# Two score matmuls side by side: the order of TensorE's work in the expert stage of an attention and mixture-of-experts kernel

## The chip, the cores and the metric

The kernel runs as one program on 1 core of a Trainium2 chip. The metric is the device time in microseconds (us), median of three runs. TensorE (PE) multiplies matrices, VectorE (DVE) and ScalarE (ACT) read its results from PSUM, GpSimd (POOL) works in SBUF, and SyncE (SP) issues the transfers. Each engine takes its own instructions in program order and waits on semaphores for the others.

## The reference

The input `x` has 2 batches of 512 rows of 128. Four residual blocks follow each other; the change lies in the second, a mixture of eight attention experts:

```python
def expert_step(acc, params):
    qw, qb_, kw, kb_, vw, vb_, ow, ob_, g = params
    q = (x @ qw.T + qb_).reshape(B, S, H, Dh).transpose(0, 2, 1, 3)   # H=16, Dh=8
    k = (x @ kw.T + kb_).reshape(B, S, H, Dh).transpose(0, 2, 1, 3)
    v = (x @ vw.T + vb_).reshape(B, S, H, Dh).transpose(0, 2, 1, 3)
    scores = jnp.einsum('bhqd,bhkd->bhqk', q, k) * scale
    p = jax.nn.softmax(scores, axis=-1)
    o = jnp.einsum('bhqk,bhkd->bhqd', p, v)
    o = o.transpose(0, 2, 1, 3).reshape(B, S, E) @ ow.T + ob_
    return (acc + o * g[..., None], None)
```

Every expert sees all rows (S = 512, E = 128) and is weighted by the router's gate `g`. The other blocks are a cross attention before it, and a cross attention and six layers of local attention with a gated feed-forward net behind it.

## The kernel before, in words

The stages run one after the other: cross attention and router to about 160 us of the profiled span, the expert stage (`stage_b_experts`) from 161 to 1239 us, then the second cross attention and the six layers to the end.

**Slots and steps.** The expert stage works through 8 experts, each in NG = 8 slots `g`; slots 0 to 3 are the first batch, 4 to 7 the second, and a slot covers 4 heads. A slot has 8 steps `s`. Queries and keys are kept as sums of bf16 parts in 48 rows (51 with the rows for the maxima). The heads of a pair (r = 0, 1) lie in rows 0 and up and rows 64 and up of the same tiles `EQX` and `EKX`.

**What TensorE does in a step**, in this order:

- `key_major` (L747): two score matmuls, keys by queries, into two of the four banks of PA. ACT takes `exp` of both at once (L832) into EPT. It waits for the `exp` of two steps before.
- `query_major` (L735): two score matmuls, queries by keys, r = 0 into the first bank of PM and r = 1 into the second. Only the row maxima are wanted of them: DVE reduces each bank to one column of ENM (`maxima`, L902). They run 14 steps ahead of the step that uses them (`LEAD`). Matmul number k waits until maximum number k - 2 is done (`pe.wait_ge(maxed, k - 1)`), which is the one that read the same bank in the step before.
- `mix` (L757): on odd steps only, four context matmuls in float32 into PV, 32 columns wide each. The profile counts eight instructions for them.
- other uses of the bank PX (`slot_uses`): in slots with g % 4 == 0 the q product after step 1 and the k product after step 2 (L696), the transposes of EON after step 5 ("ont", L144), and the output projection after step 6 ("o", L723). In slots with g % 4 == 1 the v product after step 5 (L704). In every slot the transposes of the maxima after step 3 ("rows", L144, `PX<-IDENT,ENM`) and those of the contexts after step 4 ("avt", `PX<-IDENT,EAVS`). Each waits until the use before it has left PX.

On odd steps `mix` stands between the two matmuls of `query_major`. On even steps nothing stands between them.

**Transfers.** ACT copies the transposed maxima to EROWS (L852); SP writes them into EQX with four small transfers (L590). In slots with g % 4 == 1, SP issues behind them the four transfers of `bring_in` (L582), which load EQX and EKX of the next batch from DRAM. The first `query_major` that needs them is that of step 2 of the next slot (g % 4 == 2).

Of the kernel before, what the change touches and what calls it, by code (L numbers as in the profile page):

```python
# [483 lines left out]
def slot_uses(first, last, g):  # L484

    more = not (last and g >= HG)
    u = []
    if g % HG == 0 and more:  # L490
        u += [(1, "q"), (2, "k")]
    if not (last and g == NG - 1):
        u += [(3, "rows")]
    if not (first and g == 0):
        u += [(4, "avt")]
    if g % HG == 1 and more:
        u += [(5, "v")]
    if g % HG == 0 and not (first and g == 0):
        u += [(5, "ont"), (6, "o")]
    return u  # L500
# [6 lines left out]
def use(e, g, what):  # L507

    first = isinstance(e, int) and e == 0
    last = isinstance(e, int) and e == NE - 1  # L510
    before = len(EARLY) if first else len(EARLY) - 3 + e * USES
    k = sum(len(slot_uses(first, last, i)) for i in range(g))
    return before + (k + [w for _, w in slot_uses(first, last, g)].index(what) + 1)
# [5 lines left out]
def stage_b_experts(nc, shared, d, GATE):  # L519
    with ExitStack() as ctx:  # L520
# [31 lines left out]
        def ahead(e, g, steps):  # L552

            return e + (g + steps) // NG, (g + steps) % NG

        with nc.Block() as block:
# [129 lines left out]
            def _(pe):  # L686
# [4 lines left out]
                def proj(e, b, what, n):  # L691
                    scratch(n)
                    if b == 0 and what == "q":
                        pe.wait_ge(qk_in, (e + 1) * 64)
                    w = QW if what == "q" else KW
                    pe.matmul(PX[:, :], lhsT=w[:, 0:E], rhs=XNT[:, b * S:(b + 1) * S], start=True, stop=True).then_inc(filled, 1)  # L696

                def values(e, b, n):
                    scratch(n)
                    if b == 0:  # L700
                        pe.wait_ge(v_in, (e + 1) * 16)
                    for t in range(TB):
                        k = b * TB + t
                        mm = pe.matmul(PX[:, t * 128:(t + 1) * 128], lhsT=XNT[:, k * 128:(k + 1) * 128], rhs=VW[:, :], start=True, stop=True)  # L704
                    mm.then_inc(filled, 1)

                def turn4(src, n):
                    scratch(n)
                    for t in range(TB):
                        in_ = src(t)  # L710
                        mm = turn(m, pe, PX[0:in_.shape[1], t * 128:(t + 1) * 128], in_)
                    mm.then_inc(filled, 1)

                def turn_maxima(e, g, n):
                    pe.wait_ge(max_parted, (e * NG + g) + 1)
                    turn4(lambda t: NM[:, g % 2, t, :, :].rearrange("p j s -> p (j s)"), n)

                def out_proj(e, n, b):
                    scratch(n)
                    if b == 0:  # L720
                        pe.wait_ge(o_in, (e + 1) * 16)
                    for t in range(TB):
                        mm = pe.matmul(PX[:, t * 128:(t + 1) * 128], lhsT=ONT[:, t * 128:(t + 1) * 128],  # L723
                                       rhs=OW[:, :], start=True, stop=True)
                    mm.then_inc(filled, 1)

                def query_major(e, g, s, rs=(0, 1)):
                    t, hp, b = s // 2, 2 * (g % HG) + 1 - s % 2, g // HG
                    if g % HG == 0 and s == 0 and 0 in rs:
                        pe.wait_ge(spread, (e * B + b) * SPREAD + SPREAD)  # L730
                    for r in rs:
                        k = (e * NG + g) * 16 + (2 * s + r)
                        if not (isinstance(k, int) and k < 2):
                            pe.wait_ge(maxed, k - 1)
                        pe.matmul(PM[:, r, :], lhsT=QX[64 * r:64 * r + KQ, b, hp, t * 128:(t + 1) * 128],  # L735
                                  rhs=KX[64 * r:64 * r + KQ, b, hp, :], start=True, stop=True).then_inc(qscored, 1)

                def key_major(e, g, s):
                    f = (e * NG + g) * 8 + s
                    kt, pair, b = s // 2, s % 2, g // HG  # L740
                    hp = 2 * (g % HG) + pair
                    if s == 0:
                        pe.wait_ge(rows_in, (e * NG + g) * 64 + 64)
                    if not (isinstance(f, int) and f < 2):
                        pe.wait_ge(exped, f - 1)
                    for r in range(2):
                        mm = pe.matmul(PA[:, 2 * pair + r, :], lhsT=KX[64 * r:64 * r + KS, b, hp, kt * 128:(kt + 1) * 128],  # L747
                                       rhs=QX[64 * r:64 * r + KS, b, hp, :], start=True, stop=True)
                    mm.then_inc(kscored, 1)

                def mix(e, g, kt):
                    k = e * NG + g
                    pe.wait_ge(exped, k * 8 + (2 * kt + 2))
                    if kt == 0 and not (isinstance(k, int) and k == 0):
                        pe.wait_ge(mixed_out, k)
                    for j in range(4):
                        mm = pe.matmul(PV[32 * j:32 * j + 32, :], lhsT=VP[:, g // HG, kt, 4 * (g % HG) + j, :],  # L757
                                       rhs=PT[:, kt, j * S:(j + 1) * S], start=kt == 0, stop=kt == TB - 1)
                    mm.then_inc(mixed, 1)

                def slot(e, g, first, last):
                    gp, ep = (g - 1) % NG, e - int(g == 0)
                    (e1, g1), (e2, g2), (eb, gb) = (ahead(e, g, i) for i in (1, 2, HG))

                    def scores_ahead(s, rs):
                        if s < 16 - LEAD:
                            if not (last and g == NG - 1):
                                query_major(e1, g1, s + LEAD - 8, rs)
                        elif not (last and g >= NG - 2):
                            query_major(e2, g2, s + LEAD - 16, rs)  # L770

                    def mixes(s):
                        if s == 1:
                            if not (first and g == 0):
                                mix(ep, gp, TB - 1)
                        elif s % 2 == 1:
                            mix(e, g, (s - 3) // 2)

                    for s in range(8):
                        key_major(e, g, s)  # L780
                        scores_ahead(s, (0,))
                        mixes(s)
                        scores_ahead(s, (1,))
                        for step, what in slot_uses(first, last, g):
                            if step != s:
                                continue
                            n = use(e, g, what)
                            if what in ("q", "k"):
                                proj(eb, gb // HG, what, n)
                            elif what == "avt":  # L790
                                pe.wait_ge(mixed_out, e * NG + g)
                                turn4(lambda t: AVS[:, gp % 2, t * 128:(t + 1) * 128], n)
                            elif what == "rows":
                                turn_maxima(e1, g1, n)
                            elif what == "v":
                                values(eb, gb // HG, n)
                            elif what == "ont":

                                turn4(lambda t: ON[:, gp // HG, t, :], n)
                            elif what == "o":  # L800
                                out_proj(ep, n, gp // HG)
# [8 lines left out]
                for g in range(NG):  # L810
                    slot(0, g, True, False)
                with pe.Fori(1, NE - 1) as e:
                    for g in range(NG):
                        slot(e, g, False, False)
                for g in range(NG):
                    slot(NE - 1, g, False, True)
# [861 lines left out]
```

## Time and profile before

| | |
|---|---|
| Median of 3 runs | 2467.38 us (2462.93 to 2471.3) |
| Profiled execution, span | 2469.5 us |
| PE busy over the span | 81% |
| DVE, ACT, POOL busy over the span | 71%, 59%, 42% |
| Mean granted TensorE clock | 0.908 |
| Expert stage in the span | 161 to 1239 us |

The span runs from the first to the last instruction of the one profiled execution. It is 2.1 us above the median, and it lies between the lowest and the highest of the three runs. Nothing of an execution outside its span is shown. Busy shares say where an engine works, not what it waits for; matmuls are pipelined, so that the ends of their bars overlap with the next starts, and the distance from start to start is the better measure of their cost.

### The profile page before, as it was taken

What the parts mean: (1) busy time and instruction counts of PE and PEld (TensorE: products, weight loads), DVE (VectorE), ACT (ScalarE), POOL (GpSimd) and SP (SyncE); (2) the same over time, 40 slices, a digit from 0 to 9 for tenths busy, and PEclk for the clock granted to TensorE, in tenths of its full rate; (3) what the DMA queues carried; (4) which work ended last, traced back from release to release, by engine and by line L of the source; (5) the groups of instructions that cost most, each with busy time, mean ns of one, the idle gap of its engine ahead of it and who ended that gap; (6) DMA issues with size and microseconds to landing.
All of it is one profiled execution on the core that took longest, in us unless ns stands there. A gap on an engine that the chain in (4) does not pass through costs nothing. (4 is left out here: it accounts for less than half of the span.)

```text
span 2469.5 us, 52904 instructions
## 1 busy us (share of the span) xinstructions
PE 1995.8 (81%) x18992; PEld 926.7 (38%) x18992; DVE 1761.0 (71%) x3039; ACT 1453.6 (59%) x2138; POOL 1028.3 (42%) x1009
## 2 busy tenths in 40 slices
PE   5647888888888888888847988988988988888886
PEld 3421222222222222222223554654554554555454
DVE  4736666676666666666658978878878877887794
ACT  4313556666555656555726766756757657666573
POOL 0011111111111111111039968858758767686680
PEclk9856889999899999888969998999999999999998
DMA  1022222222222222222010000000000000000000
GB/s 32 2 52 51 45 54 55 47 51 49 44 52 56 52 56 52 56 52 54 2 58 1 2 29 10 12 30 10 12 31 10 12 30 10 12 30 11 12 2 10
DMA packets 52105, 77.07 MB, mean 31 GB/s; under 512 B 10899, under 2 KB 45749, under 8 KB 48053
## 3 DMA queue, kind: packets, MB, share of 16 engines
q1 hardware_dynamic: 51317, 74.06, 13.0%
q8 instruction: 137, 2.24, 0.4%
q14 instruction: 75, 0.61, 0.1%
q10 hardware_dynamic: 576, 0.15, 0.0%
HBM read 47.70 MB, written 25.69 MB: 30 GB/s over the span
## 5 line engine op out<-in xcount | busy, mean ns | idle before, releaser
L902 DVE TENSOR_REDUCE ENM<-PM 128x1 f32<-128x512 f32 x1024 | 656.5, 685 | 335.9 <-PE PM L735 328.4
L832 ACT ACTIVATE EPT<-PA 128x1024 f32<-128x1024 f32 x512 | 520.0, 1021 | 212.0 <-PE PA L747 199.9
L735 PE MATMUL PM<-EKX,EQX 48*128 48x512 bf16 x1024 | 359.7, 414 | 177.0 <-DMA EKX<-e_park 91.0
L1216 POOL TENSOR_TENSOR DRN<-DRN,DHALF 128x8 f32<-128x8 f32 x192 | 364.5, 1899 | 7.4
L655 POOL CAST ENMP<-ENM 128x16 bf16<-128x16 f32 x64 | 12.6, 196 | 847.8 <-DVE ENM L902 847.8
L1214 POOL TENSOR_TENSOR DQR<-DR 128x512 f32<-128x512 f32 x192 | 244.2, 1272 | 246.9 <-DVE DR L1497 245.5
L735 PEld LDWEIGHTS PM<-EKX,EQX 48*128 48x128 bf16 x1024 | 83.6, 95 | 585.4 <-DVE ENM L902 404.1
L757 PE MATMUL PV<-EPT,EVP 128*32 128x512 f32 x2048 | 295.2, 651 | 0.9 <-ACT EPT L832 0.7
L747 PE MATMUL PA<-EQX,EKX 51*128 51x512 bf16 x1024 | 263.2, 404 | 5.2 <-DMA EQX<-EROWS 4.9
L1259 PE MATMUL PM<-DWQKV,DXS 128*128 128x512 f32 x384 | 216.6, 647 | 39.5 <-ACT XNT L1456 23.2
L1495 DVE TENSOR_TENSOR DR<-DRAW,DTAB 128x512 f32<-128x512 f32 x192 | 193.1, 1005 | 61.9 <-POOL DQR L1219 28.2
L1430 ACT ACTIVATE DV<-PM 64x512 f32<-64x512 f32 x384 | 225.6, 588 | 11.0 <-PE PM L1272 8.8
L1272 PE MATMUL PM<-DWQKV,DXS 128*64 128x512 f32 x768 | 213.7, 633 | 18.0 <-ACT DV L1430 14.6
L1219 POOL TENSOR_TENSOR DQR<-DQR,DRN 128x512 f32<-128x512 f32 x192 | 209.4, 1091 | 27.5
L1417 ACT ACTIVATE DRAW<-PM 128x512 f32<-128x512 f32 x192 | 114.8, 598 | 106.7 <-PE PM L1259 74.5
L144 PEld LDWEIGHTS PX<-IDENT,DQR 128*128 128x128 f32 x768 | 97.7, 144 | 101.6 <-issue 96.2
L144 PE MATMUL PA<-IDENT,DP 128*128 128x128 f32 x768 | 116.5, 295 | 18.2 <-DVE DP L1522 18.0
L1499 DVE TENSOR_REDUCE DSS<-DSQ 128x8 f32<-128x512 f32 x192 | 129.3, 674 | 0.0
L1325 PE MATMUL PV<-DWO,DOT 128*128 128x128 f32 x768 | 107.1, 297 | 22.2 <-DVE XN L1543 20.7
L1426 ACT ACTIVATE DSQ<-DRAW 128x512 f32<-128x512 f32 x192 | 121.7, 634 | 0.8
L1325 PEld LDWEIGHTS PV<-DWO,DOT 128*128 128x128 f32 x768 | 98.3, 207 | 56.2 <-issue 31.2
L144 PE MATMUL PX<-IDENT,DQR 128*128 128x128 f32 x768 | 118.5, 278 | 0.8 <-POOL DQR L1219 0.8
(204 smaller groups left out, 2930.8 us busy)
## 6 DMA issues: line engine op xcount, KB each, us to landing
e_park<-EPARTS SPq DMA_DIRECT2D x64, 192.0 KB, 2.9
EQX<-e_park SPq DMA_DIRECT2D x32, 384.0 KB, 5.6
EKX<-e_park SPq DMA_DIRECT2D x32, 384.0 KB, 9.2
DWQKV<-in_WqkvR SPq DMA_DIRECT2D x6, 1536.0 KB, 6.3
e_park<-EPARTS SPq DMA_DIRECT2D x64, 128.0 KB, 2.6
e_park<-EPARTS SPq DMA_DIRECT2D x64, 64.0 KB, 2.1
EQX<-EROWS SPq DMA_DIRECT2D x256, 3.0 KB
DWO<-in_WoR SPq DMA_DIRECT2D x6, 512.0 KB, 4.3
```

The source lines that it names most:

```text
L144: return pe.matmul(out, lhsT=in_, rhs=m.IDENT[0:k, 0:k], is_transpose=True, start=True, stop=True)
L735: pe.matmul(PM[:, r, :], lhsT=QX[64 * r:64 * r + KQ, b, hp, t * 128:(t + 1) * 128], rhs=KX[64 * r:64 * r + KQ, b, hp, :], start=True, stop ...
L747: mm = pe.matmul(PA[:, 2 * pair + r, :], lhsT=KX[64 * r:64 * r + KS, b, hp, kt * 128:(kt + 1) * 128], rhs=QX[64 * r:64 * r + KS, b, hp, :] ...
L757: mm = pe.matmul(PV[32 * j:32 * j + 32, :], lhsT=VP[:, g // HG, kt, 4 * (g % HG) + j, :], rhs=PT[:, kt, j * S:(j + 1) * S], start=kt == 0, ...
L832: s_.activation(PT[:, kt, pair * 2 * S:(pair + 1) * 2 * S], PA[:, 2 * pair:2 * pair + 2, :].rearrange("p a b -> p (a b)"), ACT.Exp, scale= ...
L902: v.tensor_reduce(NM[:, g % 2, t, j, 0:1], PM[:, r, :], AX.X, ALU.max, negate=True).then_inc(maxed, 1)
L1214: g.tensor_tensor(qr, r1, r2, ALU.add).then_inc(joined.sem, 1)
L1216: g.tensor_tensor(rn, rn, HALF[:, 0:8], ALU.pow).then_inc(rooted.sem, 1)
L1219: g.tensor_tensor(qr.rearrange("p (h e) -> p h e", h=8), qr.rearrange("p (h e) -> p h e", h=8), bc(rn, 2, [128, 8, DL]), ALU.mult).then_in ...
L1259: pe.matmul(PM[:, 0, :], lhsT=XS[:, b, W + t * 128:W + (t + 1) * 128], rhs=WQKV[:, c * 512:(c + 1) * 512], start=True, stop=True).then_inc ...
L1272: mm = pe.matmul(PM[64 * par:64 * par + 64, 1, :], lhsT=keys, rhs=wv[:, par], start=True, stop=True)
L1430: ins = s.activation(V[r, n % 4, c, :, par, :], PM[r, 1, :].rearrange("p (h e) -> p h e", h=HP), ACT.Copy)
```

## The change

On odd steps both matmuls of `query_major` are issued next to each other, and `mix` behind them. Nothing is added or left out, and even steps keep their order. The calls for the wait, the banks and the other engines stay as they are.

```diff
                     for s in range(8):
                         key_major(e, g, s)
-                        scores_ahead(s, (0,))
+                        scores_ahead(s, (0, 1))
                         mixes(s)
-                        scores_ahead(s, (1,))
                         for step, what in slot_uses(first, last, g):
```

## Rows read from the trace of the kernel before

**Rows 1.** Waits from 200 to 1290 us: total us, times, longest us.

```profile
PE PM L735 <- DVE ENM L902: 84.5, 166, 0.6
PE PM L735 <- DMA EKX<-e_park: 71.9, 15, 5.7
...
DVE ENM L902 <- PE PM L735: 305.9, 336, 6.0
```

**Rows 2.** Timeline of PE, two steps without other work: start us, us.

```profile
717.86 1.06 PE L757 MATMUL PV<-EPT,EVP 128*32 128x512 f32 x8
718.85 0.39 PE L735 MATMUL PM<-EKX,EQX 48*128 48x512 bf16 x1
718.86 0.60 PE L747 MATMUL PA<-EQX,EKX 51*128 51x512 bf16 x2
719.08 0.38 PE L735 MATMUL PM<-EKX,EQX 48*128 48x512 bf16 x1
720.03 0.39 PE L735 MATMUL PM<-EKX,EQX 48*128 48x512 bf16 x1 [0.57 <-DVE ENM L902]
...
720.62 0.39 PE L735 MATMUL PM<-EKX,EQX 48*128 48x512 bf16 x1
720.94 1.06 PE L757 MATMUL PV<-EPT,EVP 128*32 128x512 f32 x8
```

**Rows 3.** Timeline of DVE over the same two steps.

```profile
719.28 2.48 DVE L902 TENSOR_REDUCE ENM<-PM 128x1 f32<-128x512 f32 x4 [0.60 <-PE PM L735]
```

**Rows 4.** Timeline of PE, slot with g % 4 == 0, steps 1 to 7.

```profile
668.92 0.39 PE L735 MATMUL PM<-EKX,EQX 48*128 48x512 bf16 x1
...
670.55 1.12 PE L696 MATMUL PX<-XNT,EQW 128*128 128x512 f32 x2
...
671.84 0.38 PE L735 MATMUL PM<-EKX,EQX 48*128 48x512 bf16 x2
...
673.83 0.38 PE L735 MATMUL PM<-EKX,EQX 48*128 48x512 bf16 x1
...
675.45 0.60 PE L144 MATMUL PX<-IDENT,ENM 128*12 128x128 f32 x4
...
676.22 0.48 PE L735 MATMUL PM<-EKX,EQX 48*128 48x512 bf16 x2
...
677.63 0.38 PE L735 MATMUL PM<-EKX,EQX 48*128 48x512 bf16 x1
...
680.07 0.43 PE L735 MATMUL PM<-EKX,EQX 48*128 48x512 bf16 x2
...
681.99 0.38 PE L735 MATMUL PM<-EKX,EQX 48*128 48x512 bf16 x1
```

**Rows 5.** Timeline of PE, slot with g % 4 == 1, steps 5 to 7.

```profile
693.58 1.16 PE L704 MATMUL PX<-EVW,XNT 128*128 128x128 f32 x8
...
694.90 0.38 PE L735 MATMUL PM<-EKX,EQX 48*128 48x512 bf16 x2
...
696.06 0.39 PE L735 MATMUL PM<-EKX,EQX 48*128 48x512 bf16 x1 [0.56 <-DVE ENM L902]
```

**Rows 6.** Timeline of ACT, the copy that releases the transfers of `bring_in`.

```profile
690.50 0.59 ACT L852 ACTIVATE EROWS<-PX 12x512 bf16<-12x512 f32 x1 [1.28 <-PE PX L144]
```

**Rows 7.** Timeline of PE behind those transfers, at half clock.

```profile
639.39 0.61 PE L735 MATMUL PM<-EKX,EQX 48*128 48x512 bf16 x2 [5.12 <-DMA EKX<-e_park]
...
705.60 0.60 PE L735 MATMUL PM<-EKX,EQX 48*128 48x512 bf16 x2 [4.53 <-DMA EKX<-e_park]
...
706.96 0.60 PE L735 MATMUL PM<-EKX,EQX 48*128 48x512 bf16 x1 [0.34 <-DVE ENM L902]
707.49 1.93 PE L757 MATMUL PV<-EPT,EVP 128*32 128x512 f32 x8
```

**Rows 8.** Stretches of 5 us behind two stalls: length, PE busy (instructions), granted clock, DMA share, GB/s.

```profile
650.00:655.00 5.00, 4.40 (x20) 0.55 0.00 0
...
715.00:720.00 5.00, 3.89 (x24) 0.91 0.00 1
```

## The prediction

> **What bounds the kernel now.** Only the expert stage is touched, so I read its waits first [rows 1]. No engine is full there. DVE waits 305.9 us for a score matmul of `query_major` (336 times), PE waits for a maximum in turn (166 times), and 15 times PE waits some 4.8 us for EKX (71.9 us over 15). PE and DVE pass the lead to each other in a ring. The timelines of PE and DVE show the ring, and there one has to follow what starts what, not how busy anyone is.
>
> **The ring of two plain steps.** I call an even step's two matmuls e0 and e1, an odd step's o0 and o1. In [rows 2, 3]: `mix` starts at 717.86; o1 can start only behind it, at 718.85 (0.99 later). Its maximum starts at 719.28 (0.43 after o1). The four maxima of a pair of steps take 2.48 us back to back, which with a single one of 0.68 is a start every 0.60: o1's at 719.28, e0's at 719.88, e1's at 720.48. e0's ends at 720.56; o0 uses that bank and starts at 720.62 (0.06 later), and `mix` at 720.94 (0.32 later). The ring is 0.99 + 0.43 + 0.60 + 0.68 + 0.06 + 0.32 = 3.08 us, and it is what the trace shows from `mix` to `mix`. The wait of DVE for o1 (0.60) and that of PE for o1's maximum (0.57) are both in it.
>
> **What the change moves.** o1 comes in front of `mix`. It needs only its own bank, whose maximum (e1's) is one place later in DVE's order than that of e0 for which o0 waits. PE works in order, so `mix`, and behind it everything else, now waits for e1's maximum too. No operation is added and no transfer moved; o1 and `mix` keep their lengths. The new ring: `mix` starts; `key_major` 1.00 later (718.86 against 717.86); e0 and e1 together 0.22 behind it (719.08 against 718.86), since the maxima of o0 and o1 are long done by then; e0's maximum 0.43 later; e1's 0.60 after that; its end 0.68 later; o1 after 0.06; `mix` after 0.32. The sum is 3.31 us [rows 2, 3]. Against 3.08 that is **+0.22 us a plain pair**: the term of `key_major` (the hundredth above it is 718.86 for 718.85). What has happened: DVE's wait of 0.60 for o1 is gone, but instead DVE stands still during all of `mix` and `key_major`, and gets e0 as its first work. Before, o1's maximum was released one `key_major` earlier (0.22).
>
> The price of issuing o1 beside o0 where the maxima don't hold it is read where a long other use lies between the even and the odd matmuls:
>
> - **Step 1 to 3, slots g % 4 == 0** [rows 4]. e0, e1 at 671.84, o0 at 673.83: 1.99 us later. e1's maximum ends 0.43 + 0.60 + 0.68 = 1.71 after e1, so o1 costs no wait. Before, o0 to o0 is 673.83 - 668.92 = 4.91, with 0.32 for o1 between `mix` and the q product (0.99 + 0.32 from `mix`, which is 670.55 - 669.24). After, the product starts 1.00 behind `mix`. **-0.31.**
> - **Step 5 to 7, same slots** [rows 4]. e0, e1 at 680.07, o0 at 681.99, 1.92 later: the same **-0.31**.
> - **Step 3 to 5, all slots** [rows 4]. Before 677.63 - 673.83 = 3.80. After, the transposes start 0.31 earlier behind `mix`, but e0 at 676.22 and o0 at 677.63 are only 1.41 apart, and o1 needs 1.71 + 0.06 = 1.77: 0.36 of wait. **+0.05**.
> - **Step 5 to 7, slots g % 4 == 1** [rows 5]. e0 at 694.90, o0 at 696.06, 1.16 apart. After, 1.77 for o1, so 0.61 - 0.31 = **+0.30**.
> - **Where "rows" stands behind step 3**, its transposes start 0.31 nearer to `mix`; this counts only where something else than PE's order ends the stretch, as next.
>
> **The stall absorbs a part.** The transfers of `bring_in` wait for the copy of EROWS in a slot g % 4 == 1, which ends at 691.09; PE goes on at 705.60, 14.5 us later [rows 6, 7]. That length belongs to four small transfers and four large ones, not to PE. In between PE has work until 700.7 and stands about 4.8 us. What the change adds between that copy and the stall (+0.05, 0.31 for the nearer transposes, +0.30, +0.22: 0.88) only shortens the stall. So I sum from one stall's end to the next release. Behind the stall PE runs at half clock: e0, e1 at 705.60, o0 at 706.96, `mix` 0.53 later [rows 7]. There o1 waits 0.60 longer than o0 and saves its own 0.53 behind `mix`: +0.06. Then +0.05, +0.22, +0.22 to the next slot, together 0.55; the slot g % 4 == 3 gives 0.22 + 0.05 + 0.22 + 0.22 = 0.71; slot 0 gives -0.31 + 0.05 - 0.31 + 0.22 = -0.35; slot 1 up to the release +0.22 - 0.31 = -0.09. Sum: 0.55 + 0.71 - 0.35 - 0.09 = **+0.82 us**. There are 14 such stretches between 15 stalls: 11.5 us. Ahead of the first stall -0.35 - 0.09 = -0.44. Behind the last: 0.55, 0.71, a slot without q and k products 0.22 + 0.05 - 0.31 + 0.22 = 0.18, one without a v product 0.71, one pair 0.22, together 2.4; the last steps issue no `query_major`. **Sum: +13.4 us.** The profiled span of 2469.5 becomes 2482.9; the median of the runs is 2.1 below that span, so the forecast is **2481 us**, +0.5%.
>
> **The clock**, the cost that I can't place. The stretch from the stall's end (705.60) to o0 of step 7 (717.54, 0.32 before `mix` in [rows 2]) is 11.94 us, while the same work at full clock is 1.17 + 3.80 + 3.08 = 8.05: about 3.9 us lost to some 10 us at half clock [rows 7, 8], or 0.39 for each. The 1.17 is e0's maximum and the start of o0 behind it (0.43 + 0.68 + 0.06). Behind the stall that ended at 639.39 the clock was still 0.55 on the mean of 650 to 655, so half until some 654; behind the one that ended at 705.60 it is 0.91 on the mean of 715 to 720, so back at some 716 [rows 7, 8]. A stretch 3 us longer or shorter at every stall is 15 x 3 x 0.39 = 17.5 us up or down. I take no change, since at half clock PE is nearly always busy in both orders.
>
> **A rule of the skill.** In [rows 2], o1 at 718.85 and `key_major` at 718.86 start together, one in rows 64 and up, one in rows from 0: such matmuls already share the array. The Trainium skill, TensorE: Matmul & The Clock Gate, Part 3 (packing small matmuls), says that tiles in distinct row groups run concurrently, which speaks for placing o0 and o1 side by side; by it the sum would be that of the first rival. Its list of what overlaps adds that matmuls start strictly in order, which is why `mix` can't pass a waiting o1. The trace agrees with both; neither says which wait is longer, and the rows on DVE decide that.
>
> **The rivals.**
>
> - *The pair runs as one and saves PE's time everywhere* (the other side). Place: the 0.32 between o1 and what follows it. It would be 0.31 less in about 250 odd steps, -77 us: **2390 us**. For it: DVE's 305.9 us of waiting, and the pairs of [rows 4]. Against it: it holds only where e0 and o0 are 1.77 us apart, and in plain pairs they are 720.62 - 719.08 = 1.54 apart, with o0 itself waiting. Chance 0.06.
> - *The shorter stall (some 3.9 us instead of 4.8) no longer drops the clock.* That returns 3.9 us at 15 places, 58 us, against +13.4: **2422 us**. It decides if the clock row behind EKX's wait stays at 1. Nothing in the trace shows a stall of this kind without the drop. Chance 0.05.
> - *The stall doesn't shrink*, since the transfers are released later or last longer. Then the 0.88 counts 15 times more, +13: **2494 us**. Chance 0.09.
> - *No difference that can be told.* Half-clock stretches end earlier by 2 to 3 us, and take back 12 to 17 us: **2467 us**. The measurement of this kernel tells about 0.3% (7.4 us) from no change. Chance 0.20.
> - *The forecast*, 2481 us, with the clock much as it is: 2475 to 2490. Chance 0.60.
>
> **How the numbers follow.** Slower by over 0.3% (above 2474.8): 0.57 of the forecast's 0.60, and 0.09, so 0.66. Within 0.3%: the other 0.03 and 0.19 of the fourth rival, 0.22. Faster: 0.06 + 0.05 + 0.01 = 0.12. The range goes from 2465, where the half-clock stretches give back all of it and a little more, to 2498, the unshrunk stall with a quarter of the clock's bound on top; the forecast's own is 2475 to 2490.
>
> **What would show it.** Right: from `mix` to `mix` 3.30 us in plain pairs, with o1 waiting for DVE by some 0.6 behind o0; maxima in groups of four with an idle of about 0.8 before e0's, and none before o1's; 4.6 us from step 1 to 3 in slots g % 4 == 0; PE's wait for EKX about 0.9 shorter each. Wrong: plain pairs at or under 3.08 us; a clock that stays up behind the stalls, or that drops in places where it did not; a copy of EROWS that no longer ends some 14.5 us ahead of the stall's end.

## The result, and the profile after

The changed kernel takes 2473.45 us (median of 20 runs), the kernel before 2467.43 us (20 runs). The ratio is 1.0023, with a 95% interval of 1.0014 to 1.0032: 5.7 us slower, from 3.5 to 7.9. The forecast was 13.4 us slower. The direction was right, and the size less than half of what I had said. Two slow executions, one of 2834 us (the kernel before, in section 1) and one of 4180 us (the second kernel of section 2), are left out of all ratios.

The profiled execution has a span of 2470.6 us. First the waits from 200 to 1290 us (us in total, times, longest us), to be read against [rows 1]:

```profile
DVE ENM L901 <- PE PM L735: 312.0, 232, 6.0
...
PE PM L735 <- DVE ENM L901: 104.4, 318, 0.6
...
PE PM L735 <- DMA EKX<-e_park: 57.1, 15, 4.5
```

DVE waits as long as before but 232 times instead of 336: the short wait for o1 is gone and the one for e0 is longer. PE waits for maxima 318 times instead of 166. The 15 stalls are 57.1 us together instead of 71.9, so 3.8 us each instead of 4.8: they shrink by 1.0 us, where 0.88 was forecast.

The plain pair, timeline of PE, against [rows 2]:

```profile
699.91 1.07 PE L757 MATMUL PV<-EPT,EVP 128*32 128x512 f32 x8
700.91 0.39 PE L747 MATMUL PA<-EQX,EKX 51*128 51x512 bf16 x2
701.13 0.38 PE L735 MATMUL PM<-EKX,EQX 48*128 48x512 bf16 x2
701.35 0.38 PE L747 MATMUL PA<-EQX,EKX 51*128 51x512 bf16 x2
702.30 0.39 PE L735 MATMUL PM<-EKX,EQX 48*128 48x512 bf16 x1 [0.56 <-DVE ENM L901]
702.89 0.39 PE L735 MATMUL PM<-EKX,EQX 48*128 48x512 bf16 x1 [0.21 <-DVE ENM L901]
703.21 1.06 PE L757 MATMUL PV<-EPT,EVP 128*32 128x512 f32 x8
```

and of DVE, against [rows 3]:

```profile
701.55 2.48 DVE L901 TENSOR_REDUCE ENM<-PM 128x1 f32<-128x512 f32 x4 [0.82 <-PE PM L735]
```

From `mix` to `mix` it is 703.21 - 699.91 = 3.30 us, and DVE stands still for 0.82 us. The forecast was 3.31 and about 0.8. The second PE row from the end is the price: o1 starts 0.59 behind o0, and `mix` waits with it.

The slot with long products, timeline of PE, against [rows 4]:

```profile
672.62 1.06 PE L757 MATMUL PV<-EPT,EVP 128*32 128x512 f32 x8
673.61 1.13 PE L696 MATMUL PX<-XNT,EQW 128*128 128x512 f32 x2
...
676.89 0.38 PE L735 MATMUL PM<-EKX,EQX 48*128 48x512 bf16 x2
677.21 1.07 PE L757 MATMUL PV<-EPT,EVP 128*32 128x512 f32 x8
...
681.04 1.07 PE L757 MATMUL PV<-EPT,EVP 128*32 128x512 f32 x8
...
685.08 1.07 PE L757 MATMUL PV<-EPT,EVP 128*32 128x512 f32 x8
```

Step 1 to 3 takes 4.59 us (4.60 forecast), step 3 to 5 3.83 (3.85), step 5 to 7 4.04 (4.05). So in this slot every term of the ring is right to 0.02 us.

What is not as forecast stands behind the stall. Timeline of PE, against [rows 7]:

```profile
708.55 0.61 PE L735 MATMUL PM<-EKX,EQX 48*128 48x512 bf16 x2 [3.96 <-DMA EKX<-e_park]
...
709.94 1.20 PE L735 MATMUL PM<-EKX,EQX 48*128 48x512 bf16 x2 [0.35 <-DVE ENM L901]
711.07 1.93 PE L757 MATMUL PV<-EPT,EVP 128*32 128x512 f32 x8
712.94 0.95 PE L144 MATMUL PX<-IDENT,ENM 128*12 128x128 f32 x4
713.82 0.39 PE L747 MATMUL PA<-EQX,EKX 51*128 51x512 bf16 x2
...
716.13 1.06 PE L757 MATMUL PV<-EPT,EVP 128*32 128x512 f32 x8
```

The first `mix` still takes 1.93 us, at half clock (1.2 GHz). `key_major` at 713.82 already has its 0.39 of full clock (2.4 GHz), and the second `mix` takes 1.06: full clock is back within 5.3 us of the stall's end. To see whether that is one case or all, I took the 16 us behind each of the 15 stalls: length, PE busy (instructions), granted clock, DMA share, GB/s. The kernel before, the best, the worst and the median case of the 15:

```profile
512.96:528.96 16.00, 13.84 (x76) 0.84 0.02 5
...
639.39:655.39 16.00, 14.78 (x59) 0.53 0.02 5
...
900.42:916.42 16.00, 14.51 (x69) 0.69 0.02 5
```

The changed kernel, the median, the worst and the best case:

```profile
385.03:401.03 16.00, 14.43 (x74) 0.76 0.02 5
...
449.32:465.32 16.00, 14.30 (x62) 0.63 0.00 1
...
708.55:724.55 16.00, 14.23 (x76) 0.84 0.00 1
```

A mean clock c means 32 x (1 - c) us at half clock. Over 15 stalls the mean of c is 0.710 before, that is 9.3 us at half clock behind each, and 0.769 after, 7.4 us. The single cases overlap (5.1 to 15.0 us before, 5.1 to 11.8 after), so runs have to show that this is no accident of two executions.

### The profile page after: what moved, and what is told of

It is laid out like the page before. It is cut to its first block and busy times, and to the rows that moved or that the text cites. A ratio compares the mean times of both kernels' runs of the same rounds, so it can differ in the third digit from the quotient of the medians.

```text
span 2470.6 us, 52904 instructions
## 1 busy us (share of the span) xinstructions
PE 1989.3 (81%) x18992; PEld 931.2 (38%) x18992; DVE 1752.9 (71%) x3039; ACT 1435.2 (58%) x2138; POOL 1027.9 (42%) x1009
## 3 DMA queue, kind: packets, MB, share of 16 engines
q1 hardware_dynamic: 51317, 74.06, 12.8%
## 5 line engine op out<-in xcount | busy, mean ns | idle before, releaser
L901 DVE TENSOR_REDUCE ENM<-PM 128x1 f32<-128x512 f32 x1024 | 645.0, 683 | 341.5 <-PE PM L735 335.3
L831 ACT ACTIVATE EPT<-PA 128x1024 f32<-128x1024 f32 x512 | 505.8, 1020 | 192.7 <-PE PA L747 192.5
L735 PE MATMUL PM<-EKX,EQX 48*128 48x512 bf16 x1024 | 320.6, 411 | 183.0 <-DVE ENM L901 105.8
L757 PE MATMUL PV<-EPT,EVP 128*32 128x512 f32 x2048 | 286.7, 633 | 1.1 <-ACT EPT L831 0.7
L735 PEld LDWEIGHTS PM<-EKX,EQX 48*128 48x128 bf16 x1024 | 77.6, 95 | 384.3 <-DVE ENM L901 302.3
L747 PE MATMUL PA<-EQX,EKX 51*128 51x512 bf16 x1024 | 215.2, 402 | 5.2 <-DMA EQX<-EROWS 4.9
L747 PEld LDWEIGHTS PA<-EQX,EKX 51*128 51x128 bf16 x1024 | 50.1, 94 | 201.9 <-ACT EPT L831 94.2
```

What stands on the lines that cost most here:

```text
L831: s_.activation(PT[:, kt, pair * 2 * S:(pair + 1) * 2 * S], PA[:, 2 * pair:2 * pair + 2, :].rearrange("p a b -> p (a b)"), ACT.Exp, scale= ...
L901: v.tensor_reduce(NM[:, g % 2, t, j, 0:1], PM[:, r, :], AX.X, ALU.max, negate=True).then_inc(maxed, 1)
```

## The experiments

In all of them only the order on PE differs, and the work is that of the kernel before, except where said. Most keep the old order and put the pair side by side where a condition holds:

```diff
+                        together = CONDITION
                         key_major(e, g, s)
-                        scores_ahead(s, (0,))
+                        scores_ahead(s, (0, 1) if together else (0,))
                         mixes(s)
-                        scores_ahead(s, (1,))
+                        if not together:
+                            scores_ahead(s, (1,))
```

**1. Both kernels again.** No edit.

> The kernel before once more, for a second profile of it. Ratio 1.000 in both theories. Theory A (the half-clock stretches behind the 15 stalls are shorter in the changed kernel because its stalls are shorter): the half-clock time of the expert stage is near that of the first profile, some 11 us a stall, 167 us in all. Theory B (the lengths of these stretches scatter from execution to execution and have nothing to do with the change): it lies anywhere between 135 and 170 us. The time from the start of the EROWS copy to the end of the stall: 15.4 us by A and by a rival in which the transfers land faster after the change; anywhere from 15.0 to 15.4 if it scatters.

> The changed kernel once more, for a second profile. Ratio 1.0023 as measured. Theory A: half-clock time of the expert stage near the first profile of it, some 9.3 us a stall, 140 us in all, stalls of 3.8 us. Theory B: anywhere between 135 and 170 us.

The kernel before again: ratio 1.0005 (0.9989 to 1.0020). Its second profile has 9.7 us at half clock behind a stall (a mean clock of 0.697 in the 16 us), after 9.3 in the first. The changed kernel again: 1.0021 (1.0008 to 1.0034), and 7.3 us (0.773), after 7.4. The time from the start of the EROWS copy to the stall's end is 15.2 and 15.3 us on the mean, after 15.4 and 15.0 in the first profiles: that scatters and is not part of the change. The clock's difference repeats. (The two expectations count a half-clock stretch whole, with its part inside the stall; from here on I count from the stall's end, where PE has work.) It also shows in the timed executions, of which the mean granted clock over the span is known: 0.9066 on the mean of 35 executions of the kernel before, 0.9117 on that of 12 of the changed one, taken together with them, and 0.9113 on that of the 20 of its first measurement. Over 2470 us, 0.0047 to 0.0051 is 23 to 25 us less at half clock.

What that is worth can be read between cases of one kernel. From a stall's end to the `mix` of step 1 in the next slot, the kernel before takes 13.3 us where 5.1 us are at half clock and 16.8 where it is 15.0; over the 30 cases of its two profiles the time rises by 0.39 us for each us at half clock, and at 8 us the line stands at 14.39. For the changed kernel's 30 cases the slope is 0.27, and at 8 us it stands at 14.93: +0.54 at equal clock, where the sum had +0.55. (The lines are not parallel: at 7 us the difference is 0.66, at 9.3 us 0.39.) But the means are 14.97 before and 14.75 after. So the ring's price behind the stall was about right and is more than paid back by the clock: 0.76 us for each stall, 11.4 for 15.

The whole stretch that the forecast summed, from a stall's end to the copy of EROWS ahead of the next stall, takes 49.2 and 49.4 us on the mean in the two profiles before and 49.5 in both after: +0.16, where +0.82 was forecast.

**2. Where does the pair gain?** The condition is `g % HG == 0 and s in (1, 5)`, and then its complement.

> Both score matmuls side by side only at steps 1 and 5 of slots with g % 4 == 0, where a long product stands between the even step's matmuls and the odd one's; elsewhere the old order. The ring theory: -0.31 us at each of 31 places, -9.6 us, ratio 0.996, with stalls and the clock as before. Rival (a pair side by side saves nothing, the time of TensorE is not what sets the pace there): 1.000.

> The complement: side by side everywhere but at steps 1 and 5 of slots with g % 4 == 0. The ring theory with nothing else: +13.4 + 9.6 = +23 us, ratio 1.0093. With theory A (shorter stalls take back some 7 us by the clock and the transfers): +16 us, ratio 1.0065. If the small loss of the whole change comes from plain pairs costing less than 0.22 us: +6 or less, ratio 1.0025.

The first: 1.0016 (1.0001 to 1.0032), slower where 0.4% faster was expected. The second: 1.0008 (0.9996 to 1.0021) where 1.0065 or more was. One is slower than expected and the other faster, as one error on where a pair gains makes them, and the timeline of PE of the first shows it:

```profile
670.63 1.06 PE L757 MATMUL PV<-EPT,EVP 128*32 128x512 f32 x8
...
673.40 0.39 PE L735 MATMUL PM<-EKX,EQX 48*128 48x512 bf16 x1
674.00 0.39 PE L735 MATMUL PM<-EKX,EQX 48*128 48x512 bf16 x1 [0.21 <-DVE ENM L904]
674.31 1.06 PE L757 MATMUL PV<-EPT,EVP 128*32 128x512 f32 x8
...
678.89 1.06 PE L757 MATMUL PV<-EPT,EVP 128*32 128x512 f32 x8
```

`mix` to `mix` is 3.68 up to the pair at step 1, 0.60 more than 3.08, and 4.58 behind it, 0.32 less than 4.90. A pair pays its wait in the stretch that ends with it, and gains in the one that begins with it. In the changed kernel all odd steps are alike and the two fall together in every stretch, so the forecast's sum didn't need to keep them apart; in a kernel changed at some places one has to. By this count the first costs +0.28 for each stall (+0.60, -0.31, +0.35, -0.36), 4.2 us, and the second is 0.27 cheaper for each than the whole change, +9.4 us. With the clock of their timed executions (below) both agree with the measurement, the first near the lower end of its interval.

**3. The steps behind the stall.** The condition is `g % HG == 2 and s in (3, 5)`, its complement, then step 3 and step 5 alone.

> Side by side only at steps 3 and 5 of slots with g % 4 == 2, the first two odd steps behind each of the 15 stalls; the old order elsewhere. By the ring these places cost next to nothing (+0.06 at step 3; at step 5 a wait of at most 0.36, given back by 0.37 in the plain pair behind it): together within +1 us. Theory A, as it now stands (the order of work right behind the stall brings the full clock back some 2 us sooner, as all profiles so far show: 9.3, 9.7 and 8.9 us after the stall's end with the old order there, 7.4, 7.2 and 7.1 with the new one): clock back after some 7.3 us, 15 x 2 x 0.35 = 10 us saved, ratio 0.996. Theory B (the clock's return doesn't depend on this order, but on the rest of the changed kernel or on chance): back after 9.3 us, ratio 1.000.

> The complement: the changed kernel with the old order at steps 3 and 5 of slots with g % 4 == 2. Theory A: clock back some 9.3 us after the stall's end, and the full price of the ring, +13 us, ratio 1.0053. Theory B: as the changed kernel, 7.3 us and ratio 1.0023.

> Side by side only at step 3 of slots with g % 4 == 2, the first odd step behind each stall. The kernel with steps 3 and 5 so changed brought the full clock back 6.5 us after the stall's end instead of some 9, and was faster by 0.56%. If the first odd step decides that (the long wait behind the stall is followed by o0, o1 and then an unbroken run of work): most of the gain is here, ratio 0.995 to 0.997, clock back after 7 us. If the second does: ratio 1.000, clock back after some 9 us.

> Side by side only at step 5 of the same slots. If the first odd step decides: clock back after some 9 us, ratio 1.000. If the second does: clock back after 7 us, ratio 0.995 to 0.997. If each has a part: about 0.998 for both.

Steps 3 and 5: ratio 0.9944 (0.9923 to 0.9965), 13.8 us faster than before by moving some 30 matmuls. Half clock behind a stall is 6.6 us (the 16 us behind four of the stalls, as above):

```profile
382.87:398.87 16.00, 14.34 (x73) 0.78 0.02 6
446.38:462.38 16.00, 14.09 (x76) 0.84 0.00 1
509.32:525.32 16.00, 14.34 (x73) 0.78 0.02 5
572.86:588.86 16.00, 14.45 (x73) 0.74 0.00 1
```

No case of the 15 is longer than 8.3 us. The waits settle whether shorter stalls are the reason, which was theory A's in section 1:

```profile
PE PM L735 <- DMA EKX<-e_park: 67.7, 15, 5.2
```

That is 4.5 us a stall. The second profile of the kernel before has 4.7 (70.1 in all) with 9.7 us at half clock, this one 6.6. So the stall's length isn't what decides. The timeline of PE shows a second gain, that of the ring:

```profile
707.57 0.55 PE L735 MATMUL PM<-EKX,EQX 48*128 48x512 bf16 x2
708.05 1.06 PE L757 MATMUL PV<-EPT,EVP 128*32 128x512 f32 x8
...
710.43 0.39 PE L735 MATMUL PM<-EKX,EQX 48*128 48x512 bf16 x1 [0.20 <-DVE ENM L904]
710.75 1.06 PE L757 MATMUL PV<-EPT,EVP 128*32 128x512 f32 x8
```

The pair at step 5 costs no wait, since at half clock the even matmuls and the odd ones lie far enough apart, and the stretch behind it is 2.70 us instead of 3.08. The complement: 1.0053 (1.0033 to 1.0073), as theory A had said, but not for its reason alone: its profile has 7.8 us at half clock (between the two, and one of its 15 cases lasts beyond the 16 us that are counted), and its timed executions 0.9114, the clock of the changed kernel. The ring accounts for it: without the pair at step 5, the pair at step 7 costs its 0.60 and the whole is 0.31 for each stall worse than the changed kernel. Step 3 alone: 0.9968 (0.9953 to 0.9984); half clock 7.6 us. Step 5 alone: 0.9990 (0.9975 to 1.0004); 7.4 us in the profile, but its timed executions have the clock of the kernel before (0.9056 against 0.9071). So the gain at the clock is mostly the first step's by the timed executions, and each step has a part by the profiles, one of each. Both steps together are 5.9 us faster than the first alone, and the ring gives 5.5 of that. Which feature of the order the clock answers to isn't shown.

**4. Places where the pair has no wait**, `g % HG == 0 and s in (3, 7)`, and these together with the steps behind the stall.

> Side by side only at steps 3 and 7 of slots with g % 4 == 0, where a long product stands between the even step's matmuls and the odd ones, so that o1 has no wait. The kernel with only steps 1 and 5 so changed showed that a pair's wait (0.60 in a plain pair, 0.36 behind the contexts' transposes) is paid in the stretch that ends with the pair, and the gain comes in the next one. Ring theory: 0 before the pair, -0.31 behind step 3, -0.37 behind step 7 (mix to mix 2.71 instead of 3.08), -0.68 at each of 15.5 half experts, -10.5 us, ratio 0.9957, with the clock as before (back after 9.3 us). Rival (what is gained there is lost at the next wait, as in the kernel with steps 1 and 5): 1.000.

> Side by side at steps 3 and 7 of slots with g % 4 == 0 and at steps 3 and 5 of slots with g % 4 == 2, the old order elsewhere. Ring theory with theory A: the sum of the two, -20 us, ratio 0.992. With theory B: -10 us, ratio 0.996.

The first: 0.9993 (0.9975 to 1.0011), inconclusive by itself. The stretches are as the ring says (3.48 instead of 3.80 behind step 3, 2.71 instead of 3.08 behind step 7), except that step 5 to 7 is 4.56 instead of 4.40, so -0.53 in place of -0.68; but its executions ran at 0.9032 against 0.9077, 22 us more at half clock. Its profile doesn't show that (8.2 us behind a stall, less than the kernel before), so where they lost it is open. The second: 0.9919 (0.9897 to 0.9941), 20 us faster, as expected. Its order behind the stall is that of steps 3 and 5 above, and so is its half clock, 6.7 us, though one case reaches 11.8.

**5. What stands between `mix` and e0.** Three kernels, in all of which `query_major` goes first on even steps: the changed kernel with this edit, then one with the old order on all odd steps, then one with the old order only at steps 3 and 5 of slots g % 4 == 2. The edit of the first, against the changed kernel:

```diff
-                        key_major(e, g, s)
-                        scores_ahead(s, (0, 1))
-                        mixes(s)
+                        if s % 2 == 0:
+                            scores_ahead(s, (0, 1))
+                            key_major(e, g, s)
+                        else:
+                            key_major(e, g, s)
+                            scores_ahead(s, (0, 1))
+                            mixes(s)
```

> The changed kernel, and on even steps query_major is issued before key_major. The ring theory says that the changed kernel's plain pair costs 0.22 more than before because key_major stands between mix and e0; with it behind e1 the pair is 3.08 again, step 3 to 5 is 3.62 instead of 3.84 and step 5 to 7 with the v product 4.17 instead of 4.39, while the gains at the long products stay. Per stretch between two stalls about -1.8 us against before, -27 us, ratio 0.989 with the clock's return at 7.3 us as in the changed kernel. Rival (the price of the pair is the second maximum's wait of 0.60, wherever key_major stands; or the later key_major delays the exponentials): plain pairs at 3.30 or more, ratio 1.002 or more.

> The kernel before, with query_major ahead of key_major on even steps only; odd steps keep mix between o0 and o1. The ring theory: o1's maximum leads the ring there, and e0 is not waited for, so nothing changes in plain pairs (3.08) nor at the long products: ratio 1.000, although the same edit on top of the changed kernel gave 1.1%. Rival (the even order is a gain by itself): 0.99 to 0.995.

> The changed kernel with query_major ahead of key_major on even steps (0.9898 of before), with the old order at steps 3 and 5 of slots with g % 4 == 2. Theory A (the order behind the stall decides when the clock returns): back after some 8.8 us instead of 6.5, 15 x 2.3 x 0.35 = 12 us slower, ratio 0.994 to 0.995. Theory B: no difference, 0.990.

The changed kernel with this: 0.9898 (0.9874 to 0.9921), 2441.03 us, the fastest of all, 25 us under the kernel before. The timeline of PE:

```profile
652.89 1.07 PE L757 MATMUL PV<-EPT,EVP 128*32 128x512 f32 x8
653.89 0.39 PE L735 MATMUL PM<-EKX,EQX 48*128 48x512 bf16 x2
...
655.66 0.39 PE L735 MATMUL PM<-EKX,EQX 48*128 48x512 bf16 x1 [0.21 <-DVE ENM L905]
655.97 1.06 PE L757 MATMUL PV<-EPT,EVP 128*32 128x512 f32 x8
```

e0 starts 1.00 behind `mix`, and the pair is 3.08 us. This is the direct test of the forecast's term of 0.22: it was `key_major`, and goes when `key_major` goes. Step 3 to 5 is 3.62 and step 5 to 7 with the v product 4.17, both as expected. Not as expected is step 5 to 7 in slots g % 4 == 0: 4.60, where the changed kernel has 4.20 and the kernel before 4.40, so that gain did not stay. The stalls are 71.0 us in sum, as long as before, and half clock behind them is 6.5 us.

The kernel before with this: 0.9967 (0.9946 to 0.9988), not 1.000. Its plain pairs are 3.08 to 3.10, so the ring is as before; its timed clock is 0.9124 against 0.9071, and the profile has 6.8 us at half clock behind a stall: again a gain at the clock and not in the ring. (One case lasts beyond the 16 us counted.)

The third: 0.9942 (0.9921 to 0.9963), 0.44% slower than without the old order at those steps. The number is the one expected, but whether by theory A's reason isn't shown. Half clock is 6.5 us behind a stall in both profiles, but here one of the 15 cases fills the whole 16 us and goes on:

```profile
564.84:580.84 16.00, 15.22 (x60) 0.50 0.00 1
```

The profiled execution, 2446 us, is also among the fastest of the ten (2445 to 2467), and the timed clocks do differ, 0.9063 against 0.9102. The ring alone would give most of the loss: without the pair at step 5, step 5 to 7 is 3.68 instead of 3.09, 0.59 at each of 15 stalls, 9 us of the 11. With the timed clocks' difference, worth some 7, that is more than was measured, so the share of each is open.

**6. The opposite: `mix` cut in two.** For three of the four key tiles its columns 0 to 255 are computed on the odd step and 256 to 511 between e0 and e1 of the next even step. The part of the edit in `mix`:

```diff
+                    at, n = (0, S) if len(halves) == 2 else (256 * halves[0], 256)
                     for j in range(4):
-                        mm = pe.matmul(PV[32 * j:32 * j + 32, :], lhsT=VP[:, g // HG, kt, 4 * (g % HG) + j, :],
-                                       rhs=PT[:, kt, j * S:(j + 1) * S], start=kt == 0, stop=kt == TB - 1)
+                        mm = pe.matmul(PV[32 * j:32 * j + 32, at:at + n], lhsT=VP[:, g // HG, kt, 4 * (g % HG) + j, :],
+                                       rhs=PT[:, kt, j * S + at:j * S + at + n], start=kt == 0, stop=kt == TB - 1 and 1 in halves)
```

> The opposite of the change: mix is cut into two halves of 256 columns for three of four key tiles, the first between o0 and o1 as before, the second between e0 and e1 of the next even step; the mix of step 3 stays whole. By the ring, TensorE then never keeps DVE waiting for a whole mix: from o0, half mix 0.50, o1, key_major, e0, half mix, e1, and DVE's four maxima at 0.60 set the pace: plain pair 2.6 instead of 3.08, some 7 of them outside the stall's shadow in each stretch, -3.2 us, -45 us in all, ratio 0.982; the stalls grow by what is gained in their shadow. Rival (each half costs as much as a whole, since four float32 passes are needed either way and the width is not what counts): plain pair 3.1 or more, ratio 1.00 or above.

The ratio is 1.0128 (1.0096 to 1.0159), far from 0.982. The timeline of DVE:

```profile
649.77 2.48 DVE L913 TENSOR_REDUCE ENM<-PM 128x1 f32<-128x512 f32 x4 [0.17 <-PE PM L735]
652.43 2.48 DVE L913 TENSOR_REDUCE ENM<-PM 128x1 f32<-128x512 f32 x4 [0.17 <-PE PM L735]
```

The plain pair is 2.66 us, so the ring did what was said. What ate it stands in the waits (its row for EKX) and in the timeline of PE:

```profile
PE PM L735 <- DMA EKX<-e_park: 90.9, 15, 8.1
```

```profile
594.35 0.39 PE L735 MATMUL PM<-EKX,EQX 48*128 48x512 bf16 x1
598.20 0.61 PE L747 MATMUL PA<-EQX,EKX 51*128 51x512 bf16 x2 [3.47 <-issue]
...
602.69 2.07 PE L696 MATMUL PX<-XNT,EQW 128*128 128x512 f32 x2
```

The stalls are 19 us longer in sum; PE pauses five times for 3.2 to 3.7 us with nothing that it waits for, 17 us in all, which no other profile here has; and the program behind the expert stage, which is unchanged, takes 1248 us instead of 1231. Each of the five pauses stands ahead of `key_major` of step 0 in slot 0 (the q product comes after step 1), so where the loop over the experts, `pe.Fori(1, NE - 1)`, jumps back: six rounds and five jumps. Behind each the clock is at half: the q product takes 2.07 us instead of 1.12. Behind the expert stage there are four more, one a layer, of 5.1 to 5.5 us with nothing waited for, where the kernel before has none above 2.4. Why a jump costs this program 3.5 us and the others less than 2 isn't known, nor what the rest of the last 17 us is. The timed clock is 0.8975 against 0.9071, 54 us more at half clock, worth 19 us by the factor below.

**The account.** Can two terms, the ring and the clock, give all these times? The table has every kernel but the last, whose pauses are a third term. The ring, at equal clock, is what its stretches gain or lose for each stall, times 15 (for the changed kernel it is the forecast's sum; for the others the terms were read from the profiles). The timed executions' mean clock is turned into time at half clock over the whole span and counted at 0.35 us for each us (between the slopes 0.27 and 0.39). Then comes their sum, and the measured difference (ratio less 1, times 2467). The changed kernel's own clock is compared with the 35 executions of section 1.

| kernel | ring for each stall | ring us | clock before, this | us at half clock | x 0.35 | sum | measured |
|---|---|---|---|---|---|---|---|
| changed | the forecast's sum | +13.4 | 0.9066, 0.9113 | -22 | -7.8 | +5.6 | +5.7 (3.5 to 7.9) |
| steps 1, 5 of g % 4 == 0 | +0.28 | +4.2 | 0.9066, 0.9087 | -9 | -3.2 | +1.0 | +3.9 (0.2 to 7.9) |
| all but those | 0.27 less than changed | +9.4 | 0.9066, 0.9115 | -24 | -8.4 | +1.0 | +2.0 (-1.0 to 5.2) |
| behind the stall | +0.60 - 0.53 - 0.37 | -4.5 | 0.9077, 0.9120 | -24 | -8.3 | -12.8 | -13.8 (-19.0 to -8.6) |
| all but those | 0.31 more than changed | +18.0 | 0.9077, 0.9114 | -16 | -5.7 | +12.3 | +13.1 (8.1 to 18.0) |
| steps 3, 7 of g % 4 == 0 | -0.53 | -8.0 | 0.9077, 0.9032 | +22 | +7.6 | -0.4 | -1.7 (-6.2 to 2.7) |
| both choices | -0.53 - 0.30 | -12.5 | 0.9077, 0.9138 | -34 | -11.7 | -24.2 | -20.0 (-25.4 to -14.6) |
| step 3 only | +0.60 - 0.53 | +1.0 | 0.9071, 0.9102 | -16 | -5.7 | -4.7 | -7.9 (-11.6 to -3.9) |
| step 5 only | -0.37 | -5.5 | 0.9071, 0.9056 | +7 | +2.4 | -3.1 | -2.5 (-6.2 to 1.0) |
| changed, even first | +0.07 - 0.18 - 0.32 - 0.18 + 0.20 - 0.31 | -10.8 | 0.9071, 0.9102 | -20 | -6.9 | -17.7 | -25.2 (-31.1 to -19.5) |
| before, even first | +0.20, stretches longer by 0.02 to 0.09 | +3.0 | 0.9071, 0.9124 | -28 | -9.7 | -6.7 | -8.1 (-13.3 to -3.0) |
| even first, old behind the stall | changed, even first, - 0.07 + 0.59 | -3.0 | 0.9071, 0.9063 | +2 | +0.5 | -2.5 | -14.3 (-19.5 to -9.1) |

Ten of twelve sums lie in the measured interval; the ring alone has three there. The factor 0.35 and all rings but the first were set knowing the profiles, so this shows that the two terms suffice for the ten, not that they were foreseen. The factor is soft, too: among the 35 timed executions of the kernel before, the time rises by only 0.25 us for each us at half clock, and with 0.25 nine sums lie in their interval, the changed kernel's, +7.9, at its edge. The two that don't are those with the changed order and `query_major` first on even steps; both are 7 to 12 us faster than the account, and that is open. One weakness of the account bears on it: it takes the clock over the whole span. In the profile of the changed kernel with the even step's order, half clock inside the expert stage is 40 us less than in the two profiles before (194 against 231 and 238), outside it 12 and 16 us more, and there it costs next to nothing: the part behind the stage takes 1232 us, after 1231. With the stage's clock alone the sum would be -24.8. But these are single profiles, and the same reckoning for step 5 only gives -15 against the measured -2.5; so it is a hint and no answer.

## Why the prediction was wrong

- **The ring and its price.** Right. 3.30 us for 3.31, `key_major` as the term of 0.22 shown by moving it away (3.08).
- **The gains at the long products**, -0.31. Right at step 1 to 3 (-0.32). At step 5 to 7 it is -0.20 as the median over 14 stretches (4.40 to 4.20), though -0.32 in the slot shown. **Step 3 to 5** is 3.83 or 3.84 for 3.85, **step 5 to 7 with the v product** 4.39 for 4.41.
- **The stall absorbs a part.** Right: 0.88 forecast, 1.0 and 0.6 in two pairs of profiles; the time from the copy to the stall's end stays 15.0 to 15.4 on the mean.
- **Behind the stall.** The ring's +0.55 is +0.54 at equal clock (8 us).
- **The clock.** This is the step that failed: "I take no change, since at half clock PE is nearly always busy in both orders." The changed order has 2 us less at half clock behind each stall (9.3 and 9.7 against 7.4 and 7.3 in four profiles), and the mean clocks of 35 and 32 executions say the same for the whole span. That is 8 us of the 13.4 by the account, and 11.4 by the stretches of the profiles; from a stall's end to the next copy of EROWS +0.16 us came of +0.82. That PE is busy nearly all the time in both orders did not keep the clock's return where it was. I had its size in the bounds (17.5 us either way) and a rival for it, with 0.20.
- **The base.** The profiled execution lies above the median of its kernel by more than the 2.1 us that I took: spans leave out some 1.8 us that the time has (2470.6 against 2472.36 in the changed kernel's). This changes neither sum nor ratio.
- **The rivals.** A pair that saves PE's time everywhere didn't occur; the stall still drops the clock each time; the stalls did shrink. The result lies between the forecast and the fourth rival, whose half-clock stretches end earlier by 2 us, as happened; only they gave back about 8 us and not the 12 to 17 that it had.

Shown: the ring's terms, the shorter time at half clock, and the worth of both to within the factor. Not shown: why this order brings the clock back sooner. Steps 3 and 5 alone suffice for it, undoing them doesn't undo it, moving `query_major` on even steps has it too, and the length of the stall isn't the reason.

## What to carry to other kernels

Two engines that hand two buffers to and fro form a ring; write down its terms in order, and for every instruction moved ask which term it leaves and which it enters. Here the move cost 0.23% by itself and gained 1% together with a second one that took `key_major` off the ring, of which the second alone gained 0.33%. A pair pays its wait ahead of itself and gains behind itself, so a change can be kept only where the wait is free. And a kernel whose TensorE stalls at a fixed place should be tried with several orders of the work right behind the stall: reordering two of every 16 odd steps there was worth 0.56%, a third of it by the ring.

## What the runs showed of the hardware that I had not expected

- The time at half clock behind a stall depends on the order of the same work: 9.3 and 9.7 us in the old order, 6.6 and 6.7 in two kernels with two steps changed behind the stall. It scatters within one execution: from 5.1 to 15.0 us in the old order, from 5.1 to 8.3 and to 11.8 in those two, and in three other orders single cases last beyond 16 us.
- An order that is slower by the ring may be faster by the clock: the mean clock of a kernel's timed executions, 0.903 to 0.914 among the kernels of the account, moves the time by as much as the ring does.
- Cutting `mix` into two halves brought five pauses of some 3.4 us on PE with nothing waited for, each where the loop over the experts jumps back, and 17 us in a part of the program that was not changed.
